# Six buffers for slices of Wk, the row term's weights summed at the end of the projection, and the steps of one batch's statistics and row terms moved

## The reference

```python
def attention(text, features):
    Q = einsum('btx,dx->btd', text, Wq) + bq
    K = einsum('bpx,dx->bpd', features, Wk) + bk
    attn = softmax(einsum('btd,bpd->btp', Q, K) / sqrt(1024))
    return einsum('btp,bpd->btd', attn, features)

def ffn(x):                      # 4-bit weights, packed 8 to an int32
    w = (qweight >> shifts) & 15
    zeros = ((qzeros >> shifts) & 15) + 1
    weights = scales[g_idx] * (where(w > 0, 1, -1) - zeros[g_idx])
    return x @ weights + bias

x = x + attention(layernorm(x), ctx_4096)
x = x + ffn(layernorm(x))
```

## Time and profile before

| | |
|---|---|
| median of 3 runs | 583.08 us (582.61 to 584.75) |
| profiled execution | 584.93 us, its span 583.1 us |
| mean granted clock of TensorE | 0.994 |
| TensorE busy | 568.4 us, 97% of the span, 2798 matmuls |
| VectorE, ScalarE, GpSimd busy | 390.8, 217.6, 187.4 us (67%, 37%, 32%) |
| mean transfer rate | 161 GB/s, 94.01 MB |

### The profile page before, as it was taken

One profiled execution on the slowest core, in us unless ns is written; L12 is line 12 of the kernel. 1 busy time (PEld: TensorE's weight loads), 2 busy tenths in 40 slices (PEclk: granted clock), 3 DMA queues, 4 the chain that ended last, 5 costly groups with the idle time before them and its releaser, 6 DMA issues.

```text
span 583.1 us, 7565 instructions
## 1 busy us (share of the span) xinstructions
PE 568.4 (97%) x2798; PEld 469.4 (81%) x2798; DVE 390.8 (67%) x627; ACT 217.6 (37%) x410; POOL 187.4 (32%) x135
## 2 busy tenths in 40 slices
PE   8999999997999999999999999999999999999997
PEld 7778888885677777877888999988788888888886
DVE  4687866587998897784214555594997767668442
ACT  6684354311232342242427665655132032122210
POOL 2053000000000000000225966677846733742630
PEclk9989999999899999999999999999999999999999
DMA  7852100259556845743343799896312311310111
GB/s 225 230 208 74 36 1 0 73 176 310 163 164 239 283 181 139 231 171 133 120 168 157 271 350 367 322 414 247 122 44 103 144 75 71 146 72 1 72 73 72
DMA packets 39027, 94.01 MB, mean 161 GB/s; under 512 B 3096, under 2 KB 17440, under 8 KB 36816
## 3 DMA queue, kind: packets, MB, share of 16 engines
q1 hardware_dynamic: 32464, 87.25, 41.4%
q10 hardware_dynamic: 6528, 6.29, 5.0%
HBM read 59.98 MB, written 33.55 MB: 160 GB/s over the span
## 4 chain that ended last, share of the span: by engine, by line
PE 82%; DVE 8%; DMA 4%; ACT 3%; issue 2%; SPq 1%; POOL 0%; DVEq 0%; ACTq 0%
PE bank L1158 21%; PE bank L1160 21%; PE bank L1159 21%; PE bank L1202 4%; PE bank L1208 4%; PE bank L1205 4%; DMA wk_stage<-in_L_xattn_Wk 3%; PE bank L1326 2%; PE bank L1258 2%; DVE stats L840 2%; DVE junk L923 1%; DMA xin<-in_x 1%; DVE xres L1029 1%; ACT wk_hi L544 1%; PE bank L1241 1%
## 5 line engine op out<-in xcount | busy, mean ns | idle before, releaser
L1158 PE MATMUL bank<-xT_hi,m_hi 128*128 128x512 f32 x256 | 105.1, 411 | 0.0
L1160 PE MATMUL bank<-xT_hi,m_lo 128*128 128x512 f32 x256 | 101.3, 396 | 0.0
L1159 PE MATMUL bank<-xT_lo,m_hi 128*128 128x512 f32 x256 | 101.2, 395 | 0.0
L1112 DVE TENSOR_TENSOR xres<-xres,bank 128x512 f32<-128x512 f32 x56 | 38.4, 685 | 45.9 <-PE bank L1160 45.8
L519 POOL TENSOR_TENSOR l_lo_s<-l_sum_s,l_hi_s 128x512 fp32r<-128x512 f32 x32 | 42.4, 1360 | 71.2 <-DVE l_sum_s L1048 71.2
L488 POOL TENSOR_TENSOR pairs<-mv,pairs 128x2 f32<-128x2 f32 x16 | 11.1, 697 | 168.4 <-DVE mv L845 167.9
L703 ACT ACTIVATE t_pair<-bank,ucol 128x512 f32<-128x512 f32 x32 | 22.0, 688 | 115.1 <-PE bank L1160 115.0
L505 POOL TENSOR_TENSOR tT_lo<-t_pair,tT_hi 128x1024 fp32r<-128x1024 f32 x16 | 39.2, 2464 | 77.6 <-ACT tT_hi L544 77.6
L1158 PEld LDWEIGHTS bank<-xT_hi,m_hi 128*128 128x128 f32 x256 | 48.5, 190 | 12.7 <-issue 0.5
L1160 PEld LDWEIGHTS bank<-xT_hi,m_lo 128*128 128x128 f32 x256 | 48.4, 189 | 11.4
L1159 PEld LDWEIGHTS bank<-xT_lo,m_hi 128*128 128x128 f32 x256 | 48.4, 189 | 11.3 <-issue 0.2
(11 more groups left out here) (144 smaller groups left out, 1271.7 us busy)
## 6 DMA issues: line engine op xcount, KB each, us to landing
cin<-in_ctx SPq DMA_DIRECT2D x8, 1024.0 KB, 5.6
xres<-in_x SPq DMA_DIRECT2D x8, 1024.0 KB, 11.3
out<-xres SPq DMA_DIRECT2D x15, 512.0 KB, 2.7
right_scratch<-part_hi SPq DMA_DIRECT2D x28, 256.0 KB, 2.2
xn_scratch<-xin SPq DMA_DIRECT2D x6, 1024.0 KB, 4.9
xq<-xn_scratch ACTq DMA_DIRECT2D x24, 256.0 KB, 5.4
r_tile<-right_scratch SPq DMA_DIRECT2D x6, 1024.0 KB, 11.5
xin<-in_x SPq DMA_DIRECT2D x5, 1024.0 KB, 7.2
```

The lines of the kernel that those rows point to most:

```text
L1112: dve.tensor_tensor(part, part, prod_bank(f, n)[:, :], ALU.add).then_inc(s_acc, 1)
L1158: pe.matmul(out_, a_hi, b_hi, start=start, stop=False, skip_group_check=True)
L1159: pe.matmul(out_, a_hi, b_lo, start=False, stop=False, skip_group_check=True)
L1160: return pe.matmul(out_, a_lo, b_hi, start=False, stop=stop, skip_group_check=True)
```

## The change

- `wk_stage` has six buffers, the two new ones in memory of `m_lo` that is written later. The load of slice c waits for slice c - 6. The load of Wq block 2 is issued before slice 7's load, not before slice 5's.
- `w_row` is issued behind the last projection and transposes, before step 0 of the T stage. VectorE's two copies of the u sums (`copy_u`) stand before `x_lo(0, 5)`.
- VectorE does `x_stats(2)` behind the row terms of batches 0 and 1.
- Batch 4: statistics in step 5 instead of 4, normalisation in 6 instead of 5 (with its store, and the load of batch 6's raw rows), row terms in step 9 instead of 5, by a table of their own. Batch 5: statistics in 10 instead of 9. The blocks of batch 4 are transposed in step 12 instead of 10.
- ScalarE, in the scores of batch 1: `p_hi(0)` before `t_hi(2, 0)`.

```diff
-        wk_stage = [at(f"wk_stage{i}", 146.25 + 4 * i, [P, D], F32) for i in range(4)]
+        N_STAGE = 6
+        wk_stage = [at(f"wk_stage{i}", kb, [P, D], F32) for i, kb in enumerate((146.25, 150.25, 154.25, 158.25, 34, 38))]
...
-        X_STATS = {1: 3, 4: 4, 9: 5, 12: 6, 17: 7}
-        X_APPLY = {0: 2, 2: 3, 5: 4, 11: 5, 16: 6, 18: 7}
-        X_BLOCKS = {4: 2, 6: 3, 10: 4, 14: 5, 19: 6, 22: 7}
-        RAW = {2: (4, 5), 5: (6,), 12: (7,)}
+        X_STATS = {1: 3, 5: 4, 10: 5, 12: 6, 17: 7}
+        X_APPLY = {0: 2, 2: 3, 6: 4, 11: 5, 16: 6, 18: 7}
+        X_ROWS = {0: 2, 2: 3, 9: 4, 11: 5, 16: 6, 18: 7}
+        X_BLOCKS = {4: 2, 6: 3, 12: 4, 14: 5, 19: 6, 22: 7}
+        RAW = {2: (4, 5), 6: (6,), 12: (7,)}
...
-                if c == 5:
+                if c == NB - 1:
                     load_wq(2)
-                if c >= 4:
-                    sp.wait_ge(s_wklo, c - 3)
-                    sp.wait_ge(s_wkbq, c - 3)
-                sp.dma_start(wk_stage[c % 4], wk_rows[:, c, :]).then_inc(s_wkl[c % 4], 16)
+                if c >= N_STAGE:
+                    sp.wait_ge(s_wklo, c - N_STAGE + 1)
+                    sp.wait_ge(s_wkbq, c - N_STAGE + 1)
+                sp.dma_start(wk_stage[c % N_STAGE], wk_rows[:, c, :]).then_inc(s_wkl[c % N_STAGE], 16)
...
                     if b == 1:
+                        p_hi(0)
                         t_hi(b + 1, 0)
-                        p_hi(0)
                     t_hi(b + 1, 1)
...
+            def copy_u():
+                dve.wait_ge(s_u, 1)
+                dve.tensor_copy(ucol, bank[4][:, 0:2 * NB].rearrange("p (j two) -> p j two", two=2)[:, :, 0]
+                                ).then_inc(s_cons, 1)
+                order.link(dve.tensor_copy(bsum[:, 1:2], bank[4][:, 2 * NB:2 * NB + 1]))
+                dve.sem_inc(s_cons, 1)
...
                 if b == NB - 1:
-                    for u in range(6):
+                    for u in range(5):
                         x_lo(0, u)
+                    copy_u()
+                    x_lo(0, 5)
...
-            x_stats(2)
             row_terms(0)
             row_terms(1)
+            x_stats(2)
...
                     if n in X_APPLY:
                         x_apply(X_APPLY[n])
-                        row_terms(X_APPLY[n])
+                    if n in X_ROWS:
+                        row_terms(X_ROWS[n])
...
+                        if c == NB - 1:
+                            w_row()
...
-                    if n == 0:
-                        w_row()
```

More of the change, by code:

```diff
@@ L188, in xattn_ffn_kernel @@
         s_wq0 = [sem(f"half_of_wq_block{i}_loaded") for i in range(2)]
-        s_wkl = [sem(f"wk_loaded{i}") for i in range(4)]
+        s_wkl = [sem(f"wk_loaded{i}") for i in range(N_STAGE)]
         s_wkhi, s_wklo0, s_wklo = sem("wk_hi"), sem("half_of_first_wk_lo"), sem("wk_lo")
@@ L561, in times_bq @@
                 wait(act, s_uacc, c - 4)
-                act.activation(wk_bq[c % 4] if c else uacc, wk_stage[c % 4], ACT.Copy, scale=bcols[:, 0, c:c + 1]
+                act.activation(wk_bq[c % 4] if c else uacc, wk_stage[c % N_STAGE], ACT.Copy, scale=bcols[:, 0, c:c + 1]
                                ).then_inc(s_wkbq, 1)
@@ L580, in _ @@
                     wq_split(1, 1)
-                act.wait_ge(s_wkl[c % 4], 16 * (c // 4 + 1))
-                copy(wk_hi[:, c, :], wk_stage[c % 4]).then_inc(s_wkhi, 1)
+                act.wait_ge(s_wkl[c % N_STAGE], 16 * (c // N_STAGE + 1))
+                copy(wk_hi[:, c, :], wk_stage[c % N_STAGE]).then_inc(s_wkhi, 1)
                 if c == NB - 1:
@@ L790, in wk_split @@
                 dve.wait_ge(s_wkhi, n_hi)
-                return dve.tensor_tensor(wk_lo[:, c, cols], wk_stage[c % 4][:, cols], wk_hi[:, c, cols].bitcast(F32),
+                return dve.tensor_tensor(wk_lo[:, c, cols], wk_stage[c % N_STAGE][:, cols], wk_hi[:, c, cols].bitcast(F32),
                                          ALU.subtract)
@@ L908, in _ @@
             x_lo(0, 7)
[L909 to L913, removed]
             def row_terms(b):
@@ L1212, in proj, with w_row @@
                         ins.then_inc(s_wqused, 1)
+            def w_row():
+                pe.wait_ge(s_wacc, NB)
+                pe.wait_ge(s_cons, 3)
+                for h in range(2):
+                    pe.matmul(bank[4 + h][:, :], ones2[:, 0:1].broadcast_to([P, P]), wacc[:, h * HALF:(h + 1) * HALF],
+                              start=True, stop=True).then_inc(s_wr, 1)
             for c in range(NB):
```

## The result

| | before | changed |
|---|---|---|
| median | 582.85 us (581.90 to 584.75, 4 runs, the three above and one more) | 574.74 us (573.88 to 574.92, 4 runs) |
| profiled execution | 584.93 us, span 583.1 | 574.79 us, span 573.0 |
| mean granted clock of TensorE | 0.994 | 0.999 |

The ratio of the times is 0.985 (95% interval 0.983 to 0.988). The change is faster by 8 to 10 us. The two profiled executions differ by 10.1 us, and the forecast made this difference 10.2; the medians shown here differ by 8.1. Over all executions on record, 65 of the kernel before and 10 of the changed one, the medians are 583.2 and 574.3, which is 8.9.

The account below looks back on a forecast made before the run. TensorE, busy 568.4 of 583.1 us, bounds the kernel; its waits and low clock can be won. Terms -3.6 - 0.6 - 5.9 + 0.5 - 0.6 = -10.2 take 584.93 to 574.7, less 1.85 is 572.9 us; range 571.0 to 577.2.

Parts of the forecast that it names:

- the likeliest case: The prediction's own forecast for the whole kernel, 572.9 us, with a range of 571.2 to 574.5; chance 0.63.
- The tables: Steps 4 to 9: the weights half is ready before TensorE's gather; -5.9 us, 4.4 of wait and 1.5 of clock.
- The one-hot wait: Before the gather: VectorE comes 1.8 us sooner up to step 4, so the one-hot matrix is in time; -0.6 us.
- `p_hi`: ScalarE in the scores: pT_hi(0) goes ahead of a tT_hi and is 0.9 sooner, shortening a TensorE wait; -0.6 us.
- The price in steps 9 to 16: VectorE runs later with moved work, so TensorE waits slightly at gathers and the border to pair 2; +0.5 us.
- Six buffers: Projection: slice 7 of Wk loads sooner, so TensorE's wait goes; -3.6 us, some 1.9 wait and 1.7 clock.
- From the profile to the median: Whole kernel: the runs' median lies 1.85 us below the profiled execution, so 574.7 becomes 572.9 us.
- A: Step 4: the transpose waits for batch 2's reloaded blocks, TensorE waits 3.1 us; gain 5.6, 577.5 us; chance 0.10.
- B: Steps 9 to 16: VectorE later, two 1 us waits, one followed by low clock; gain 7.1, 576.0 us; chance 0.15.
- C: Somewhere else: one clock drop without a wait of its own costs 1.6; gain 8.6, 574.5 us; chance 0.06.
- D: Slice 7 or gather: one wait stays through a second cause; gain 4.3 to 6.6, 576.5 to 578.8 us; chance 0.04.
- E: Step 10: splits wait for later stores, delaying VectorE's line, gathers 3 to 5 and pair 2; slower, 586 us; chance 0.02.

Follow-up runs that it names:

- the second measurement: The changed kernel, unedited, measured once more on the third chip beside the kernel before: 574.25 us (6 runs), ratio 0.9826.
- the third chip: Chip of the third group of experiments: the kernel before took 584.26 us there (11 runs), the changed kernel 574.25 us (6 runs).
- before, again: The kernel before, unchanged, run and profiled a second time: 583.44 us (12 runs), ratio 1.0006; its profiled execution took 585.46 us.
- queue held: The kernel before, with SyncE's queue held behind the load of slice 7 of Wk until that landed: 582.86 us, ratio 0.9996.
- `w_row` alone: The kernel before with only w_row at the projection's end, earlier copies of the u sums, and x_stats(2) behind the row terms: 580.87 us, ratio 0.9957.

## Why the prediction was right, and where it was off

The time, 574.74 us, lies in the range (571.0 to 577.2), and faster, which had 0.95. It lies 1.8 us above the point, and just outside the likeliest case's own range (571.2 to 574.5); the second measurement (574.25) lies within that. By its steps:

- **The tables, -5.9.** The size held: alone they give 5.6 us, and VectorE had 3.0 us to spare at the gather for 3.2 forecast. But its 1.5 us for the clock had the wrong cause. The forecast counted the stream to 150.51 and looked no further; at the next gather VectorE would have made TensorE wait for them in any case, clock or no clock. They were won because the row terms of batch 4 left the place between the two halves of the weights. Undone, the tables cost 4.2 to 4.6, not 5.9: with `w_row` moved, the first wait they remove is 3.1 us and no longer 4.3, and the second is 1.3. The two edits share one wait. In either order they add up to about the same (2.1 and 4.2, or 5.6 and 0.9), and to the 6.5 of the forecast.
- **The one-hot wait, -0.6.** Held: 0.6 in the view of waits, 0.9 in the time.
- **`p_hi`, -0.6.** Held: 0.66 to 0.2 in the trace, 0.7 in the time.
- **The price in steps 9 to 16, +0.5.** Too high: no wait at the gather (0.18 us of slack was left), under 0.1 us at the border to pair 2. Of the 1.3 us of added work, idle time took 0.9 (1.77 less 0.86) instead of the 0.65 allowed.
- **Six buffers, -3.6.** This is the step that failed. The wait did go, and in the profiled pair the projection won 3.0 us, near the 3.6 less the 0.8 that the start happened to wait longer. But over the executions the part is worth 0.8 to 1.2 us, alone and undone. Three of six profiles with four buffers had a wait of 1.7 us or more for slice 7, one of 0.9, two none, and only one of the six had low clock behind it. The forecast took 1.9 of wait and 1.7 of clock as certain.
- **From the profile to the median, -1.85.** This is the same error once more. The profiled execution of before stood 1.85 us above its median, and it had waited 1.77 us for slice 7 and lost 1.7 of clock behind it, which no other of the six profiles with four buffers did; that of the changed kernel stands 0.05 above its own. So the excess went with the change, and may not be counted as a gain and also be subtracted at the end. That slice 7 is all of the excess is not shown. From span to span the sum is right (10.2 forecast, 10.1 found), which is in part luck: both ends are single executions. Against the medians it is 2.1 us too much for the pair shown, 1.3 over all executions and 0.2 on the third chip, where the kernel before took 584.26. The steps give 1.9 to 2.3: 3.6 less the 0.8 to 1.2, less the 0.4 of the price and the 0.1 of `p_hi`.

The rivals: of A, the transpose at step 4 did not wait for batch 2's reload; the 1.39 us of batch 3's are hidden. B, C, D and E show in no view: no wait over 1 us between steps 9 and 19, no low clock from 10 to 565 us (the stretch from 565 to 573, in which TensorE runs out of work, has 0.92), neither of the two waits left, no store behind which VectorE lost its place. That the median (574.74) still came where C would put it (574.5) is luck; what moved it there is the size of the first term.

## What to carry to other kernels

A wait for a load in one profile is a draw from a spread: before pricing it, look at a second profile of the same kernel, or at how far the profiled execution stands above the median, and don't subtract that excess from a sum whose terms were read from the excess. A wait for an engine that works through a list in order (here 4.3 us, in both profiles of the kernel before) can be priced to a few tenths, and two edits that shorten the same wait are worth their union. Follow both engines to their next meeting: if the late engine is late there too, time that the other loses in between, to the clock or to anything else, is free, and winning it back alone gains nothing. The largest gain here came from putting work with far-off readers behind the two halves of the weights for which TensorE stood.

## What the runs showed of the hardware

- **Behind waits of 1.7 to 3.1 us, whether a low clock follows varies.** Four waits between 1.7 and 3.2 us stand in front of dense matmuls: 1.77 us (before), 1.74 (four buffers again), 2.84 (before, again) and 3.14 (old tables); behind the first the clock was 0.52 for 3.4 us, behind the others 1.00. Behind the longer waits at the gather it fell in all five profiles that have one: 4.3 us twice (before), 4.1 twice (six buffers alone, queue held) and 3.3 (`w_row` alone). It stayed low for 3.4 us in two of the five and for 6.8 in three. The Trainium skill (TensorE: Matmul & The Clock Gate, Part 1) says that the moment of the switch varies from run to run when the clock rises at the start of steady work; here its fall varied too, and for the shorter waits whether it came at all.
- **What it costs depends on who is late next.** Between the two gathers of the old tables, where VectorE is the limit, the distance was 7.47 us without a low stretch, 7.48 (before) and 7.58 (`w_row` alone) with 3.4 us of it, and 8.41 (before, again), 8.21 (six buffers alone) and 8.95 (queue held) with 6.8. So the first 3.4 us cost 0.1 at most and the rest 0.7 to 1.5. Over the 61 executions of the kernel before in the experiments none had a mean clock above 0.997. The 24 with 0.997 took 582.6 us on average, the 33 with 0.993 or 0.994 took 583.7, and the 4 with 0.990 or 0.991 took 587.5. Part of a low stretch can also fall into the wait itself, as in the stretch of 143.0 to 146.4 above, where TensorE did nothing and the clock was 0.80.
- **The load of one slice (512 KB), behind the same loads, started ScalarE anywhere from 25.4 to 28.4 us**, 3.6 to 7.0 us after its issue, and holding back what stands behind it in the queue did not change the median (582.86 against 583.07). With nothing else to move, the release came 1.6 us after the last packet.
